# The delta rule's last doubling level writes the transposed off-diagonal quarter straight into DT

## What is computed

```python
k = k / jnp.linalg.norm(k, axis=-1, keepdims=True)
def step(S, kv_t):
    k_t, v_t = kv_t
    u_t = v_t - jnp.einsum('nc,ncd->nd', k_t, S)
    S = S + k_t[:, :, None] * u_t[:, None, :]
    return (S, u_t)
_, u = jax.lax.scan(step, S0, (k.transpose(1, 0, 2), v.transpose(1, 0, 2)))
kv = jnp.einsum('ntk,ntv->nkv', k, lr * u)
y = jnp.einsum('nsk,nkv->nsv', q, kv)
```

## Time and profile before

| what | value |
|---|---|
| median of 3 runs | 2485.64 us |
| the runs | 2484.41, 2485.64, 2489.68 us |
| the profiled execution, its own time | 2487.36 us |
| its span, first to last instruction | 2485.6 us |
| mean granted TensorE clock | 0.942 of full speed |
| delta stage, levels and bodies | about 120 to 735 us of the span |

### The profile page before, as it was taken

The page is one execution under the profiler, slowest core; times in us unless marked ns, Lnnn a source line. Parts: engine busy times, 40 slices in busy tenths (PEclk is TensorE's granted clock), DMA queues, the critical chain, the costliest instruction groups (busy, mean ns, idle before and its releaser), DMA issues. The chain is left out here.

```text
span 2485.6 us, 58427 instructions
## 1 busy us (share of the span) xinstructions
PE 2206.9 (89%) x22066; PEld 1952.9 (79%) x22066; DVE 1611.4 (65%) x4117; ACT 1085.9 (44%) x2678; POOL 719.9 (29%) x553
## 2 busy tenths in 40 slices
PE   7789989899988188988699999998699999999999
PEld 3488879898868078888577777776599999999998
DVE  1655545455545945565589999998666666676674
ACT  2433333233323055555256666665244444444443
POOL 0000000000000275551067777775312112121120
PEclk9889999999995588999799999999799999999999
DMA  8000000000003021110000000000000000000000
GB/s 195 7 1 1 1 2 1 2 1 1 1 19 88 21 56 38 41 37 14 1 3 3 3 3 3 3 3 2 1 8 13 7 13 6 7 13 6 13 7 14
DMA packets 42038, 40.91 MB, mean 16 GB/s; under 512 B 7720, under 2 KB 35784, under 8 KB 41416
## 3 DMA queue, kind: packets, MB, share of 16 engines
q1 hardware_dynamic: 35912, 25.66, 4.1%
q0 software_dynamic: 5888, 12.07, 1.9%
HBM read 25.30 MB, written 12.41 MB: 15 GB/s over the span
## 5 line engine op out<-in xcount | busy, mean ns | idle before, releaser
L1898 ACT ACTIVATE w<-banks,b 128x384 f32<-128x384 f32 (+1 forms) x512 | 259.7, 573 | 393.1 <-PE banks L1972 393.1
L1954 PE MATMUL banks<-w,w 128*128 128x128 f32 (+1 forms) x3072 | 364.2, 275 | 0.0
L1954 PEld LDWEIGHTS banks<-w,w 128*128 128x128 f32 (+1 forms) x3072 | 350.4, 189 | 9.2 <-issue 8.7
L1489 PE MATMUL banks<-qT,w 64*64 64x128 f32 x4608 | 274.4, 272 | 14.8 <-DVE eb L1392 12.2
L1489 PEld LDWEIGHTS banks<-qT,w 64*64 64x64 f32 x4608 | 251.5, 134 | 29.9 <-DVE eb L1392 17.0
L1497 PE MATMUL banks<-eb,w 64*64 64x128 f32 x4608 | 272.4, 271 | 0.7 <-DVE eb L1392 0.7
L1799 DVE SCALAR_TENSOR_TENSOR h<-banks,t_wt,h 128x128 f32 (+3 forms) x672 | 183.7, 341 | 117.1 <-PE banks L1954 114.3
L1497 PEld LDWEIGHTS banks<-eb,w 64*64 64x64 f32 x4608 | 249.2, 133 | 1.3 <-DVE eb L1392 1.0
L1457 POOL TENSOR_TENSOR t<-eb 128x768 f32<-128x768 f32 x96 | 175.7, 1830 | 137.3 <-ACT eb L1437 125.3
L1392 DVE TENSOR_TENSOR eb<-eb,rd 128x1536 f32<-128x1536 f32 x96 | 211.5, 2203 | 1.6 <-ACT rd L1446 1.6
L1069 POOL DMA_INDIRECT xg<-xs,rowu x184 | 180.0, 978 | 104.1 <-issue 53.6
(11 more groups left out here) (285 smaller groups left out, 4632.3 us busy)
## 6 DMA issues: line engine op xcount, KB each, us to landing
out<-h SPq DMA_DIRECT2D x16, 320.0 KB
xs<-r_xl SPq DMA_DIRECT2D x16, 192.0 KB, 2.8
h<-in_xT SPq DMA_DIRECT2D x4, 750.0 KB, 15.4
h<-in_xT SPq DMA_DIRECT2D x4, 749.0 KB, 18.3
xg<-xs,rowu POOLq DMA_INDIRECT x184, 2.5
xs<-r_xl SPq DMA_DIRECT2D x16, 128.0 KB
w<-in_L_ffn_w1T SPq DMA_DIRECT2D x1, 1024.0 KB
xs<-r_xl SPq DMA_DIRECT2D x16, 53.0 KB
```

Source lines behind the costliest of these rows:

```text
L1489: last = nc.tensor.matmul(lbanks(n)[place(n, hd), v, :], k.Kt[half(hd), v, :], qT[half(hd), n // NC % 2, (n % NC) * P:(n % NC + 1) * P], s ...
L1898: nc.scalar.activation(gb[u % 2][:, f, s * GW:s * GW + NFREE[s]], k.ps[:, order.bank(n), 0:NFREE[s]], ACT.Relu, bias=k.b1_1[:, 2 * e + f:2 ...
L1954: last = nc.tensor.matmul(k.psf[0:n, o:o + P], gb[u % 2][:, f, c * P:c * P + n], k.w2_1[:, 2 * e + f, :], start=(f == 0), stop=(f == 1))
```

## The change

At level 6 TensorE takes W as weights (64 columns) and the right half of DT, 64 columns per chunk, as the moving operand, so that the product arrives already transposed, on 64 partitions. ScalarE copies it with scale -1 into the upper right quarter of DT (64 partitions, 6 times 64 columns), in place of the 128x768 copy. The level's subtraction on VectorE and the 12 transposes on TensorE are dropped. The semaphore counts follow: `d_ready` and `t_ps` count 2*NL per pair, `dt_ready` still 2*LV.

```diff
--- before.py
+++ after.py
@@ -479,16 +479,15 @@
                 def levels(i, first, last_pair):
                     for par in range(2):
                         masked(i, 1, par)
-                    for lv in range(1, LV):
+                    for lv in range(1, NL):
                         s = LEVELS[lv - 1]
                         for par in range(2):
                             dve.wait_ge(x_ps, i * (2 * NL) + ((lv - 1) * 2 + par + 1))
                             d = left(flat(seq(D, par)), s)
                             nc.vector.tensor_tensor(d, d, k.ps[:, par * 4 + 1, 0:GW].rearrange("p (q t) -> p q t", t=s),
                                                     ALU.subtract).then_inc(d_ready, 1)
-                        if lv < LV - 1:
-                            for par in range(2):
-                                masked(i, lv + 1, par)
+                        for par in range(2):
+                            masked(i, lv + 1, par)
                         if lv in (1, 2) and not last_pair:
                             for g in (2 * lv - 2, 2 * lv - 1):
                                 dve.wait_ge(turned, i * 4 + (g + 1))
@@ -597,10 +596,15 @@
                     nc.scalar.activation(seq(D, par), bc(k.ident[:, :], NC), ACT.Copy).then_inc(reset, 1)
 
                 def levels(i, last_pair):
-                    for lv in range(LV):
+                    for lv in range(NL):
                         for par in range(2):
-                            act.wait_ge(t_ps, i * (2 * LV) + (lv * 2 + par + 1))
+                            act.wait_ge(t_ps, i * (2 * NL) + (lv * 2 + par + 1))
                             nc.scalar.activation(by_bank(DT, par), two_banks(par), ACT.Copy).then_inc(dt_ready, 1)
+                    for par in range(2):
+                        act.wait_ge(x_ps, i * (2 * NL) + ((NL - 1) * 2 + par + 1))
+                        nc.scalar.activation(seq(DT, par)[0:HALF, :, HALF:P],
+                                             k.ps[0:HALF, par * 4 + 1, 0:GW].rearrange("p (c t) -> p c t", t=HALF),
+                                             ACT.Copy, scale=-1.0).then_inc(dt_ready, 1)
                     if not last_pair:
                         for par in range(2):
                             unit(par)
@@ -679,7 +683,7 @@
                         last.then_inc(gram_ps, 1)
 
                 def turn(i, lv, par):
-                    pe.wait_ge(d_ready, i * (2 * LV) + (lv * 2 + par + 1))
+                    pe.wait_ge(d_ready, i * (2 * NL) + (lv * 2 + par + 1))
                     for c in range(NC):
                         last = nc.tensor.transpose(k.ps[:, par * 4 + 2 + c // GC, (c % GC) * P:(c % GC + 1) * P],
                                                    D[:, par * NC + c, :], k.ident[:, :])
@@ -706,12 +710,16 @@
                             pe.wait_ge(dt_ready, i * (2 * LV) + ((lv - 1) * 2 + par + 1))
                             for c in range(NC):
                                 m = par * NC + c
-                                last = nc.tensor.matmul(k.ps[:, par * 4 + 1, c * HALF:(c + 1) * HALF],
-                                                        DT[:, m, :], W[:, m, :], start=True, stop=True)
+                                if lv < NL:
+                                    last = nc.tensor.matmul(k.ps[:, par * 4 + 1, c * HALF:(c + 1) * HALF],
+                                                            DT[:, m, :], W[:, m, :], start=True, stop=True)
+                                else:
+                                    last = nc.tensor.matmul(k.ps[0:HALF, par * 4 + 1, c * HALF:(c + 1) * HALF],
+                                                            W[:, m, :], DT[:, m, HALF:P], start=True, stop=True)
                             last.then_inc(x_ps, 1)
-                        for par in range(2):
-                            turn(i, lv, par)
-                            if lv < LV - 1:
+                        if lv < NL:
+                            for par in range(2):
+                                turn(i, lv, par)
                                 n_d(lv + 1, par)
 
                 def body(i, p, before_last, last_pair):
```

## The result

The changed kernel takes 2459.97 us (median of 6 runs, 2457.50 to 2461.49), and the kernel before 2485.02 (6 runs, 2480.49 to 2495.16). The ratio is 0.9891, with a 95% interval of 0.9870 to 0.9912: faster by 25 us, where I had said 23. The profiled executions lie further apart than the medians, 2487.36 against 2457.50, so 29.9 us. Neither can be read as the size of the change, as the stages that it does not touch differ by more than a few us from run to run. What repeats to a few tenths is the delta stage from its first body to its last.

A forecast was written before the change was run, and what follows sets the result against it. TensorE's chain was taken to bound the delta stage, with level 6's tail exposed. Six plain pairs at 2.98 us and two jump pairs at 2.56 sum to 23.0 us off the 2485.64 median: 2462.6 us, range 2458 to 2474.

The forecast's parts named there:

- the tail of a plain pair: Level 6 of the six plain pairs, up to TensorE's next transposes: 2.98 us sooner per pair.
- the copy: ScalarE's new 64x384 copy at level 6: takes 0.49 us, bounds 0.41 and 0.81.
- the start of L717's par 1: Level 6 loads of the second sequence: wait for the mask ending at 410.17 us, start 0.05 later at 410.22.
- The spacing of the narrow loads: Level 6 weight loads of 64 columns: start 0.056 us apart in place of 0.112.
- narrow weights are cheaper: Main case, level 6 matmuls: 64-column loads take half the spacing, 0.056 us; 2462.6 us in all, chance 55%.
- The rival with a spacing of 0.112: Level 6 loads: narrow weights no cheaper, plain pairs gain 1.84 us each, 2471.6 us in all; chance 32%.
- L709 would gain nothing: Level 6 matmuls: by the skill's rule load and pass come one after the other, giving 2471.6 us.
- The rival with one record after another: Level 6's 24 matmul records: spacing 0.275 us, 17 us slower in all, 2502 us; chance 4%.
- The rival with the instruction stream at every pair's end: End of each pair: TensorE's late code ends the wait, perhaps 5 us gained, about 2480.5 us; chance 6%.
- The 5.17 and 2.48 us themselves stay, as the jump stays.: Outer loop's jump back: both TensorE instruction waits keep their length; only the last loads before it end 2.56 us sooner.
- the two pairs themselves: The two 80.0 us pairs with the outer jump: gain 2.56 us each, to near 77.4.
- The clock rival: Delta or a later stage: four more clock falls cost 19 us, about 2482 us stay; chance 3%.

The follow-up runs named there:

- E7: The changed kernel with only TensorE's loop over the pairs written out, so no jump back in its stream; 2441.34 us, 0.9822 of the kernel before.
- E9: The kernel before with TensorE's loop over the pairs written out, on another chip; 2564.33 us, 0.9946 of the kernel before.
- E1: The changed kernel with the last level's matmul weights widened from 64 to 128 columns, extra result rows not read; 2471.58 us.
- E5: The changed kernel run again, unaltered, as control; 2457.13 us, 0.9887 of the kernel before.
- E12: The changed kernel run again, unaltered, on another chip; 2547.60 us, 0.9891 of the kernel before.
- E3: The changed kernel with 12 idle transposes issued once by TensorE ahead of the delta stage; 2466.79 us.
- E4: The kernel before with 6 idle transposes issued once by TensorE ahead of the delta stage; 2481.07 us.
- E2: The kernel before with ScalarE's last-level copy cut to the upper right quarter of each transposed chunk, all else kept; 2482.72 us.

## Why the prediction was right in part, and which step was off

**Right: the tail of a plain pair.** The forecast was 2.98 us; plain pairs in the loop gained 2.89 (71.98 to 69.09), and the seven-pair lengths without jumps give 2.84 on average. Its terms held one by one: the copy 0.48 for 0.49, the start of L717's par 1 behind the mask and not behind par 0, TensorE 0.14 behind the last copy for 0.13. The spacing of the narrow loads is (1.56 - 0.14)/23 = 0.062 on average with the pause between the sequences, and 0.058 within a sequence, for 0.056. Of the missing 0.09, 0.07 is the start of par 1's loads 0.12 behind the mask, where I had put 0.05; in E7, where it is 0.05, five of the seven pairs gain 2.95 to 3.00 against E9. The late start at the change of width is not part of it, as par 1 waits for the mask anyway.

**Right: narrow weights are cheaper.** The rival with a spacing of 0.112 is refuted by the 1.56 us of L717, and E1 shows its 1.05 us a pair by taking the narrowness away. The rule of the Trainium skill that I weighed ("TensorE: Matmul & The Clock Gate", section "The mechanism": a load overlaps a running matmul only in another row group) does not hold for these matmuls. If load and pass came one after the other, 0.112 would be a whole load and a pass and 0.058 half a load and the same pass, which leaves 2 x 0.058 - 0.112 = 0.004 us for a pass of 64 columns. (The same section also has loads pulled ahead when they go to the background weight buffer; no run here shows whether that is the case.) My step from that rule to "L709 would gain nothing" was wrong as well: by it too the load's share of the 2.76 us would have halved. The rival with one record after another falls with the same row. The rival with the instruction stream at every pair's end falls too, since all plain pairs gained.

**Wrong: "The 5.17 and 2.48 us themselves stay, as the jump stays."** This is the step that failed. The two jumps cost the kernel before 518.5 - 501.8 = 16.7 us and the changed kernel 492.8 - 481.9 = 10.9, so they gave back 5.8 us that I did not count (6.0 with the 492.6 of the first profile). For the two pairs themselves I had 2 x 2.56 = 5.1 us and near 77.4 us each, and they gained 11.3 and took 75.3 and 73.0. The seven-pair length shrank by 25.9 us, 19.9 of it from the data path and 6.0 from the jumps. With the eighth level that makes 8 x 2.84 + 5.8 = 28.5 us. The whole stage (first normalisation to the router's first matmul) shrank from 619.1 to 590.4 us, by 28.7, but so close an agreement is chance, as the same changed kernel had 588.5 us in E5 and 591.1 in E12.

I had kept the length of a wait because its cause, the jump, was kept. But the second wait belonged to how much code lay ahead of the loop's head (by my reading, to where the head lay in a fetched block), and the change had taken 12 transposes out of it. E3 puts a like number back and brings the second wait back with them; E4 removes it from the kernel before with 6 transposes that do nothing. The wait at the jump itself shrank by 1.2 us each (5.17 to 3.96 at the first); E2 shows that it moves with TensorE's code unchanged, and what sets it I have not settled. E3 says how far the placement goes: with 12 idle transposes the seven-pair length of the changed kernel goes from 492.6 to 496.4 us, so 3.8 of the 6.0 us are luck of the placement and no merit of the change; with other code ahead of the loop the same edit might have got none of them. The other 2.2 us stay open: they go with the shorter wait at the jump, and whether the shorter loop of the changed kernel has a part in it no run tells.

**The total.** By this account the kernel should gain 28.5 us, and the medians say 25 with an interval of 22 to 32; 23.0 lies in it as well. The total alone would have let my forecast pass as right for the wrong reason. The clock rival did not come about: the stage's granted clock is 0.97 to 0.98 before and after, and the stages behind it vary by themselves: from the last body's start to the end the kernels other than E9 to E12 took 1765 to 1781 us, with the same code there in all of them.

## What to carry to other kernels

When one result is needed transposed, look whether the matmul that makes it can take its operands in the other roles: it saves the transpose, the step that waits for it, and here half the weight load, as the narrow operand becomes the weights. Price a wait on the instruction stream by itself, and expect that it can change with instructions put in or taken out ahead of it; a few idle instructions ahead of a loop, or a written-out loop, tell what it is worth. And where the whole varies more than the change, find a pair of rows around the changed place that repeats to a few tenths in runs of the same kernel, and compare that. A longer stretch that takes in an unsteady part, as the start of this stage, can agree with an account by chance.

## What was not expected of the hardware

- Behind a jump back, TensorE stood 5.17 us and, two loads later, another 2.48 us, or 3.96 and 0.99, or 3.82 and nothing. The second of the two waits comes and goes with the number of instructions ahead of the loop. The branch itself lasted 4.6 to 4.9 us at the three jumps with two 16 KB blocks of instructions in it, and 3.3 to 3.9 at the 15 with one. A jump cost 8.3 us in the kernel before and 5.5 in the changed one, all told.
- Going from weights of 128 columns to weights of 64, the first load came 0.26 us after the load before it, where with equal widths (E1) it is 0.11; so this change of width delays the load by 0.15 us. The way back, from 64 to 128, was not measured.
- Loads of 64 columns against 64 moving columns follow each other by 0.058 us where those of 128 columns take 0.112, at the same granted clock of 1.00.
- On two chips (E5 and E12) the changed kernel had the same seven-pair length within 0.1 us, while its median as a whole was 90 us longer on the second.
